# One-hots of a recommendation tower moved to GpSimd, between its gathers

## The chip, the cores and the metric

The kernel runs on 1 core of a Trainium2 chip. The metric is the device time of one execution in microseconds (us), the median of several runs. The core has a matrix engine (PE), a vector engine (DVE), a scalar engine (ACT), GpSimd (POOL) and SyncE (SP), which here only issues transfers.

## The reference

Inputs are 512 samples, each with 16 dense values and 50 ids into 50 tables of 1000 to 125000 rows of 16 floats. For each sample the 50 rows are fetched, the inner products of all 1225 pairs of them are taken, and a three-layer perceptron runs on them:

```
e = stack([tbl_f[ids[:, f]] for f in range(50)], axis=1)      # (512, 50, 16)
gram = einsum('bid,bjd->bij', e, e); z = gram[:, I_IDX, J_IDX]  # pairs i < j
h = concatenate([z, dense_ctx], axis=1)                         # (512, 1241)
h = maximum(h @ W_top1 + b_top1, 0)                             # 512 wide
h = maximum(h @ W_top2 + b_top2, 0)                             # 256 wide
y = h @ W_top3                                                  # (512, 1)
```

Everything is float32.

## The kernel before, in words

The 512 samples are 4 tiles (0 to 3) of 128. A field gets its row in one of three ways.

**Small tables** (26 fields, NS; at most 1280 rows) lie in SBUF as `table`, 128 partitions by R = 10 rows of 16. The id is split into a quotient (the partition) and a remainder. The quotients of all samples are written to DRAM and read back to every partition as `wide` (`load_wide(t)` on SP, two buffers, tile t in t % 2). A comparison of `wide` with the partition's own number, `consts[:, 0:1]`, gives the one-hot matrices `onehot[:, t % 2, field, :]` (128x128 each, `onehots(t, u)`, L510, on DVE, nine fields at a time: three instructions a tile, the last with eight fields). PE multiplies one-hot by table for three fields at a time (`select(t, u)`, L777, u from 0 to 8). DVE multiplies the result with a mask of the remainder (`pick`, L498) and sums it (`fold`, L482) into `fixed`.

**Two large tables** (NP = 2) go by one-hots too, in tiles 1 to 3, four matrices each (`onehots_large(t, n)`, L519; `select(t, 9)` and `select(t, 10)`, L767).

**The other large tables** are gathered row by row from DRAM by GpSimd's indirect DMA: 24 gathers in tile 0 and 22 in each of tiles 1 to 3, 90 in all, each with 128 samples of one field, into `moving`. Each tile's first 12 are its mid part (the gathers 1 to 12, 25 to 36, 47 to 58 and 69 to 80), the others its late part (tile 2's end with gather 68). Tile 3's late part is cut into three, so that the work can begin on each. Behind every gather GpSimd clears a piece of memory that nobody reads, `spacer`, 128x288 (L300):

```
    if ticks[0]:
        pool.wait_ge(spaced, ticks[0])
    nc.gpsimd.memset(spacer[:], 0.0).then_inc(spaced, 1)
    ticks[0] += 1
```

**Products.** For each tile DVE transposes the small fields (`turn_smalls`, L536), the mid part (`turn_mid`, L542, waits for `mid_gathered[t]`) and the late part (`turn_late`, L558). DVE and ACT copy them onto block diagonals (`copy_mid`, `copy_late`, and on ACT `raise_mid`, `raise_late`, L214, L344, L356). PE multiplies (`product_y(t)`, L792, for the mid part; `product_x(t, part)`, L811, for the late one), DVE and ACT unload the result from PSUM to `z` (`unload_y`, `unload_x`, `unload_pairs`, L220, L225). The first layer is 12 chunks of 4 matmuls for a tile (`chunks`, L818), the sixth of which is the first to need the late part; then ACT's Relu (`hidden`, L383), the second layer on PE (L868, L878) and the third on DVE (`last_layer`, L604).

**The order.** Every engine works through its own instructions strictly in order, and between engines there are semaphores. The order of PE, ACT and DVE is written out by hand at the end of each engine's block (DVE L607 to L752, PE L887 to L942, ACT L392 to L424). SP's order is: the small tables, `load_wide(0)`, the other tables, `load_wide(1)`, weights, `load_wide(2)`, the two large tables, `load_wide(3)`, the rest of the dense input, the result. `load_wide(t)` for t >= 2 waits until the one-hots of tile t - 2 are made, since they read the same buffer.

Of the kernel before, what the change touches and what calls it, by code (L numbers as in the profile page):

```python
# [8 lines left out]
P = 128  # L9
# [26 lines left out]
QP = P // Q  # L36
SPACE = 288
SIDE = 64

# [22 lines left out]
WC = 3 * SC  # L62
# [7 lines left out]

CONSTS = 5 + SPLIT + RL


# [20 lines left out]
def build_tower(nc, quotients, ids, ids_t, extra, small, w1, w2, b2, w3, consts_in, out, *tables):  # L94
# [8 lines left out]
    with ctx:  # L103
# [21 lines left out]
        onehot = sb("onehot", [P, 2, NS, P])  # L125
        large_mask = sb("large_mask", [P, TILES - 1, NP, RL])
        large_hot = sb("large_hot", [P, NP, SPLIT, P])
        picked = sb("picked", [P, 3, SC, D, R])
# [34 lines left out]
        wide_ready = sem("wide_ready")  # L163
        large_ready = sem("large_ready")
        rows_made = sem("rows_made")
        rows_used = sem("rows_used")
# [68 lines left out]
        def _(sp):  # L235
# [51 lines left out]
        @block.gpsimd  # L287
        def _(pool):

            ticks = [0]  # L290

            def gather(t, slot, table, field, landed):

                nc.gpsimd.indirect_dma_start(  # L294
                    moving[:, t, slot, 0:D], None, table,
                    bass.IndirectOffsetOnAxis(ap=ids_sb[:, t, field:field + 1], axis=0),
                ).then_inc(landed, 16)
                if ticks[0]:
# [12 lines left out]
            pool.wait_ge(spaced, TILES * NL - sum(SELECTED))  # L311

        @block.scalar
        def _(act):
# [112 lines left out]
        def _(dve):  # L427
# [27 lines left out]
            def large_masks():  # L455

                dve.wait_ge(folded, unit(0, NSC))
                fields = ids_sb[:, 1:, NS + HALF:NS + HALF + NP]
                quot_l = quot[:, 1:, 0:NP]
                rem_l = rem[:, 1:, 0:NP]  # L460
                step(nc.vector.tensor_scalar(quot_l, fields, -(RL - 1) / 2, 1.0 / RL, ALU.add, ALU.mult))
# [52 lines left out]
            def onehots_large(t, n):  # L514

                dve.wait_ge(wide_loaded[t], 16)
                if SELECTED[t - 1]:
                    dve.wait_ge(rows_made, unit(t - 1, NSC + n + 1))
# [121 lines left out]
            fold(1, 1)  # L640
            fold(1, 2)
            unload_y(0)
            onehots(1, 2)
            onehots(2, 0)
            onehots(2, 1)
            onehots(2, 2)
            pick(1, 3)
            pick(1, 4)
            turn_late(0, 0)
            pick(1, 5)  # L650
            copy_late(0, 0)
            fold(1, 3)
            fold(1, 4)
            fold(1, 5)
            pick(1, 6)
            pick(1, 7)
            unload_x(0, 0)
            pick(1, 8)
            unload_pairs(0)
            fold(1, 6)  # L660
            fold(1, 7)
            pick(1, 9)
            fold(1, 8)
            fold(1, 9)
            onehots_large(2, 0)
            onehots_large(2, 1)
            turn_smalls(1)
            pick(1, 10)
            pick(2, 0)
            fold(1, 10)  # L670
            fold(2, 0)
            pick(2, 1)
            turn_mid(1)
            pick(2, 2)
            onehots(3, 0)
            copy_mid(1)
            fold(2, 1)
            fold(2, 2)
            onehots(3, 1)
            onehots(3, 2)  # L680
            pick(2, 3)
            pick(2, 4)
            fold(2, 3)
            unload_y(1)
            pick(2, 5)
            fold(2, 4)
            fold(2, 5)
            pick(2, 6)
            pick(2, 7)
            fold(2, 6)  # L690
            fold(2, 7)
            pick(2, 8)
            last_layer(0)
            fold(2, 8)
            turn_late(1, 0)
            pick(2, 9)
            copy_late(1, 0)
            pick(2, 10)
            turn_smalls(2)
            pick(3, 0)  # L700
            fold(2, 9)
            fold(2, 10)
            unload_x(1, 0)
            fold(3, 0)
            unload_pairs(1)
            pick(3, 1)
            pick(3, 2)
            fold(3, 1)
            fold(3, 2)
            onehots_large(3, 0)  # L710
            onehots_large(3, 1)
            turn_mid(2)
            pick(3, 3)
            copy_mid(2)
            fold(3, 3)
            pick(3, 4)
            pick(3, 5)
            fold(3, 4)
            fold(3, 5)
            last_layer(1)  # L720
            smalls(3, 6, 7)
# [12 lines left out]
            unload_pairs(2)  # L734
# [20 lines left out]
        def _(pe):  # L755

            def select(t, u):
# [130 lines left out]
            selections(0, 0, 9)  # L888
            selections(1, 0, 5)
            product_y(0)  # L890
            layer0 = first_layer(0)
            chunks(layer0, 4)
            select(1, 5)
            chunks(layer0, 1)
            selections(1, 6, 8)
            product_x(0, 0)
            selections(1, 8, 11)
            select(2, 0)
            chunks(layer0, 5)
            selections(2, 1, 3)  # L900
            chunks(layer0, 2)
            selections(2, 3, 5)
            second_layer(0)
            product_y(1)
            selections(2, 5, 7)
            layer1 = first_layer(1)
            chunks(layer1, 1)
            select(2, 7)
            chunks(layer1, 1)
            selections(2, 8, 11)  # L910
            select(3, 0)
            chunks(layer1, 1)
            select(3, 1)
            chunks(layer1, 1)
            product_x(1, 0)
            select(3, 2)
            chunks(layer1, 7)
            selections(3, 3, 5)
            chunks(layer1, 1)
            select(3, 5)  # L920
            second_layer(1)
            selections(3, 6, 8)
            select(3, 8)
            product_y(2)
            select(3, 9)
# [91 lines left out]
```

## Time and profile before

| | |
|---|---|
| median of 3 runs | 158.98 us (158.74 to 159.48) |
| profiled execution, own time | 159.45 us |
| its span in the profile | 157.3 us |
| busy PE, DVE, ACT, POOL | 127.8, 110.6, 44.4, 124.7 us |
| gathers (L294) | 90, busy 89.3 us |
| clearings (L300) | 90, busy 35.4 us |
| one-hots on DVE (L510) | 12, busy 10.4 us |

A profile comes from one execution, and its times are in microseconds from the start of the span. The 2.15 us between its own time and its span lie around the span. A row of the timeline gives the start, the time to the end of the group, engine, line, operation, what it writes and reads with shapes, and the number of instructions; the bracket gives how long the engine stood idle before it and what ended that.

### The profile page before, as it was taken

The numbers are of one execution on the slowest core, as the hardware profiler recorded it, in microseconds if no ns is written. First come the engines' busy times: TensorE is split into PE (matmuls) and PEld (weight loads), VectorE is DVE, ScalarE is ACT, GpSimd is POOL, SyncE is SP. The second block draws the span as 40 slices with busy tenths as digits, with TensorE's granted clock in tenths as the row PEclk, the third lists the DMA queues.
The fourth block names the chain that finished last, engine by engine and source line by source line (L and its number), as shares of the span: only waits on it lengthen the run. The fifth ranks groups of instructions, "written<-read, shape, count | busy, mean of one in ns | idle before, by whom it ended". The sixth has DMA issues, their size and how long they took to land.

```text
span 157.3 us, 3325 instructions
## 1 busy us (share of the span) xinstructions
PE 127.8 (81%) x1323; PEld 111.9 (71%) x1323; DVE 110.6 (70%) x193; ACT 44.4 (28%) x77; POOL 124.7 (79%) x184
## 2 busy tenths in 40 slices
PE   0007875937698999999999989999995994999992
PEld 0007764827588679978959989886695983899991
DVE  1807899998899989998898894999953019344021
ACT  8930000232205220332071205204422018444020
POOL 2989898898998989899889889898988898982000
PEclk9999998696899999999999999999999999999998
DMA  3199999734380010000000100010000000000000
GB/s 84 35 358 419 442 417 317 279 116 119 125 256 15 6 6 4 10 7 4 10 6 4 10 4 6 11 10 6 4 10 6 4 10 4 10 6 6 0 0 1
DMA packets 6486, 12.40 MB, mean 79 GB/s; under 512 B 2077, under 2 KB 5414, under 8 KB 6342
## 3 DMA queue, kind: packets, MB, share of 16 engines
q1 hardware_dynamic: 3592, 11.46, 19.7%
q0 software_dynamic: 2880, 0.74, 5.6%
q8 instruction: 10, 0.16, 0.5%
q14 instruction: 4, 0.03, 0.1%
HBM read 12.17 MB, written 0.03 MB: 78 GB/s over the span
## 4 chain that ended last, share of the span: by engine, by line
POOL 70%; PE 14%; issue 9%; DMA 3%; ACT 2%; DVE 1%; DVEq 0%
POOL moving L294 50%; POOL spacer L300 20%; PE psm L818 4%; PE gram L811 4%; DMA moving<-tbl,ids_sb 2%; PE gram L818 2%; PE p L818 2%; DMA ids_sb<-in_ids 1%; PE gram L792 1%; PE pt L878 1%; ACT blocks L214 1%; DVE mcols L542 1%; ACT scols L344 0%; PE pt L868 0%; DVE h2w L604 0%
## 5 line engine op out<-in xcount | busy, mean ns | idle before, releaser
L294 POOL DMA_INDIRECT moving<-tbl,ids_sb x90 | 89.3, 992 | 17.4 <-issue 14.6
L777 PE MATMUL psm<-table,onehot 128*128 128x160 f32 x208 | 36.7, 326 | 19.3 <-DVE onehot L510 12.8
L777 PEld LDWEIGHTS psm<-table,onehot 128*128 128x128 f32 x208 | 32.2, 206 | 22.3 <-issue 12.8
L818 PE MATMUL p<-z,w_sb 128*128 128x128 f32 x312 | 39.3, 276 | 2.3 <-DVE z L225 2.3
L818 PEld LDWEIGHTS p<-z,w_sb 128*128 128x128 f32 x312 | 37.1, 192 | 3.6 <-ACT z L225 1.8
L300 POOL MEMSET spacer<- 128x288 f32 x90 | 35.4, 394 | 0.0
L498 DVE TENSOR_TENSOR picked<-psm,mask 128x480 f32<-128x480 f32 (+1 forms) x36 | 22.1, 634 | 4.5 <-PE psm L777 4.2
L214 ACT COPY blocks<-mcols 32x384 f32<-32x384 f32 (+3 forms) x20 | 15.4, 771 | 32.4 <-DVE mcols L542 21.2
L220 DVE COPY z<-gram 63x384 f32<-63x384 f32 (+1 forms) x20 | 9.6, 480 | 17.3 <-PE gram L811 14.0
L482 DVE TENSOR_REDUCE fixed<-picked 128x48 f32<-128x480 f32 (+1 forms) x36 | 21.3, 627 | 0.2
L767 PE MATMUL psm<-large_table,large_hot 125*128 125x400 f32 x48 | 16.9, 501 | 0.0
L220 ACT COPY z<-gram 63x384 f32<-63x384 f32 (+1 forms) x20 | 8.1, 407 | 30.5 <-PE gram L811 21.8
L510 DVE TENSOR_SCALAR onehot<-wide,consts 128x1152 f32<-128x1152 bf16 (+1 forms) x12 | 10.4, 917 | 3.9 <-DMA wide<-quotients 3.9
L767 PEld LDWEIGHTS psm<-large_table,large_hot 125*128 125x128 f32 x48 | 8.8, 190 | 5.9
L214 DVE COPY blocks<-mcols 32x384 f32<-32x384 f32 (+3 forms) x20 | 12.3, 613 | 0.7
L811 PEld LDWEIGHTS gram<-blocks,scols 128*63 128x63 f32 x384 | 11.5, 138 | 1.5 <-ACT scols L356 0.7
L811 PE MATMUL gram<-blocks,scols 128*63 128x52 f32 (+2 forms) x384 | 12.2, 216 | 0.5 <-ACT scols L356 0.5
L536 DVE STREAM_TRANSPOSE scols<-fixed 128x1632 f32<-128x1632 f32 x4 | 12.3, 3084 | 0.0
L792 PE MATMUL gram<-blocks,scols 128*63 128x48 f32 x256 | 9.5, 239 | 3.0 <-ACT scols L344 3.0
L792 PEld LDWEIGHTS gram<-blocks,scols 128*63 128x63 f32 x256 | 9.0, 155 | 4.1 <-issue 4.1
L329 ACT COPY moving<-fixed 128x192 f32<-128x192 f32 x4 | 1.4, 351 | 34.5 <-DVE fixed L482 34.5
L542 DVE STREAM_TRANSPOSE mcols<-moving 128x384 f32<-128x384 f32 x4 | 3.6, 903 | 8.4 <-DMA moving<-tbl,ids_sb 8.4
(50 smaller groups left out, 86.5 us busy)
## 6 DMA issues: line engine op xcount, KB each, us to landing
wide<-quotients SPq DMA_DIRECT2D x4, 896.0 KB, 8.2
w_sb<-in_w SPq DMA_DIRECT2D x1, 3072.0 KB, 17.4
large_table<-tbl SPq DMA_DIRECT2D x2, 781.2 KB
moving<-tbl,ids_sb POOLq DMA_INDIRECT x90, 2.8
table<-in_small SPq DMA_DIRECT2D x1, 720.0 KB, 7.2
table<-in_small SPq DMA_DIRECT2D x1, 640.0 KB, 8.7
w_sb<-in_w SPq DMA_DIRECT2D x1, 512.0 KB
table<-in_small SPq DMA_DIRECT2D x1, 480.0 KB, 5.9
```

Source lines behind the costliest of these rows:

```text
L214: return copy(blocks[QP * q:QP * (q + 1), t % 2, :, a:b, q], mcols[QP * q:QP * (q + 1), t % 2, :, a:b])
L220: return copy(to.rearrange("p k (n j) -> p k n j", n=2), g[:, 1 + a:1 + b].rearrange("p (k h) n j -> p k h n j", h=2)[:, :, h])
L294: nc.gpsimd.indirect_dma_start(moving[:, t, slot, 0:D], None, table, bass.IndirectOffsetOnAxis(ap=ids_sb[:, t, field:field + 1], axis=0),) ...
L300: nc.gpsimd.memset(spacer[:], 0.0).then_inc(spaced, 1)
L482: nc.vector.tensor_reduce(fixed[:, t % 2, UPPER + a:UPPER + b, 0:D], picked_rows(m, b - a, R), AX.X, ALU.add).then_inc(folded, 1)
L498: nc.vector.tensor_tensor(picked_rows(m, k, rows), psm[:, m % 2, 0:k * rows * D].rearrange("p (f r d) -> p f d r", r=rows, d=D), which.uns ...
L536: nc.vector.transpose(scols[:, t % 2, :, 0:MID].rearrange("p j s -> p s j"), fixed[:, t % 2]).then_inc(small_cols, 1)
L767: ins = nc.tensor.matmul(psm[:, m % 2, 0:RL * D], large_hot[0:UNITS, n, q, :], large_table[0:UNITS, n, q, :], start=q == 0, stop=q == SPLI ...
L777: ins = nc.tensor.matmul(psm[:, m % 2, (f - a) * R * D:(f - a + 1) * R * D], onehot[:, t % 2, f, :], table[:, f, :], start=True, stop=True)
L792: ins = nc.tensor.matmul(gram_out(2, WIDE, g, 1, GC), scols[:, t % 2, g, 0:WIDE], blocks[:, t % 2, g, YS:, :], start=True, stop=True)
L811: ins = nc.tensor.matmul(gram_out(0, WIDE, g, a, b), scols[:, t % 2, g, XB:], blocks[:, t % 2, g, a:b, :], start=True, stop=True)
L818: return nc.tensor.matmul(hidden_sums(t, k), w1_sb[:, c, P * k:P * (k + 1)], z[:, t % 2, c, :], start=first, stop=last)
```

## The change

Behind 35 of the 90 gathers GpSimd no longer clears `spacer` but compares two fields (256 columns) of `wide` with the partition's number and writes them to `onehot`. These are tile 1's fields 9 to 25 (behind gathers 13 to 21), all 26 of tile 2 (behind 23 to 35) and all 26 of tile 3 (behind 41 to 53). DVE keeps tile 0's three instructions and tile 1's first, fields 0 to 8. PE waits on `pool_ready` for the fields of GpSimd, and SP's `load_wide(3)` waits for the GpSimd one-hots of tile 1 in place of DVE's. The quotients and remainders of the two large tables get memory of their own. `onehots_large(t, n)` waits for PE only where the tile before used that matrix. The orders of PE, DVE and ACT are written anew. In the cut diff, a line of "..." is left out text.

```diff
+HOT_FIELDS = 2
+HOT_BEGINS = {1: 12, 2: 22, 3: 40}
+FIRST_HOT = {0: 26, 1: 9, 2: 0, 3: 0}
+VECTOR_HOTS = [3, 4, 4, 4]
+def pool_hots(t, b):
+    return sum(-(-(NS - FIRST_HOT[n]) // HOT_FIELDS) for n in range(1, t)) + -(-(b - FIRST_HOT[t]) // HOT_FIELDS) if t else 0
...
             def load_wide(t):
                 if t >= 2:
-                    sp.wait_ge(wide_ready, NWC * (t - 1))
+                    sp.wait_ge(wide_ready, VECTOR_HOTS[t - 2])
+                    if t > 2:
+                        sp.wait_ge(pool_ready, pool_hots(t - 2, NS))
                     sp.wait_ge(large_ready, sum(SELECTED[:t - 1]))
...
             def gather(t, slot, table, field, landed):
...
+                count[0] += 1
+                for tile, began in HOT_BEGINS.items():
+                    first = FIRST_HOT[tile] + HOT_FIELDS * (count[0] - 1 - began)
+                    if FIRST_HOT[tile] <= first < NS:
+                        pool_onehots(tile, first, min(first + HOT_FIELDS, NS))
+                        return
+                clear_spacer()
+
+            def pool_onehots(t, a, b):
+                if a == FIRST_HOT[t]:
+                    pool.wait_ge(wide_loaded[t], 16)
+                    if t == 1:
+                        pool.wait_ge(consts_loaded, 16)
+                    else:
+                        pool.wait_ge(rows_made, unit(t - 2, NSC))
+                nc.gpsimd.tensor_scalar(onehot[:, t % 2, a:b, :],
+                                        wide[:, t % 2, P * a:P * b].rearrange("p (f b) -> p f b", b=P),
+                                        consts[:, 0:1], None, ALU.is_equal).then_inc(pool_ready, 1)
...
-            pool.wait_ge(spaced, TILES * NL - sum(SELECTED))
+            pool.wait_ge(spaced, ticks[0])
...
# ACT
-            place_smalls(2)
             raise_late(1, 0)
             unload_x(1, 0)
+            place_smalls(2)
             unload_pairs(1)
+            hidden(1)
             raise_mid(2)
-            hidden(1)
+            unload_y(2)
             place_smalls(3)
-            unload_y(2)
...
# DVE, first part
             fold(0, 2)
+            fold(0, 3)
             pick(0, 4)
-            onehots(1, 0)
-            onehots(1, 1)
             pick(0, 5)
-            fold(0, 3)
+            onehots_large(1, 0)
...
             fold(0, 8)
+            onehots_large(1, 1)
             large_masks()
+            turn_smalls(0)
+            turn_mid(0)
+            onehots(1, 0)
+            copy_mid(0)
             pick(1, 0)
             pick(1, 1)
-            turn_smalls(0)
-            turn_mid(0)
-            pick(1, 2)
-            copy_mid(0)
-            onehots_large(1, 0)
-            onehots_large(1, 1)
...
-            onehots(1, 2)
-            onehots(2, 0)
-            onehots(2, 1)
-            onehots(2, 2)
...
-            onehots(3, 0)
...
-            onehots(3, 1)
-            onehots(3, 2)
...
# DVE, end of tile 2
             fold(3, 8)
-            unload_y(2)
+            turn_late(2, 0)
+            copy_late(2, 0)
             turn_smalls(3)
-            turn_late(2, 0)
             pick(3, 9)
-            copy_late(2, 0)
+            pick(3, 10)
+            unload_x(2, 0)
             fold(3, 9)
-            smalls(3, 10, 11)
-            unload_x(2, 0)
+            fold(3, 10)
             unload_pairs(2)
...
# PE
                 a, b = field_groups(SC)[u]
-                pe.wait_ge(wide_ready, NWC * t + -(-b // WC))
+                if b <= FIRST_HOT[t] or t == 0:
+                    pe.wait_ge(wide_ready, (VECTOR_HOTS[t - 1] if t else 0) + -(-b // WC))
+                else:
+                    if FIRST_HOT[t]:
+                        pe.wait_ge(wide_ready, VECTOR_HOTS[t])
+                    pe.wait_ge(pool_ready, pool_hots(t, b))
...
             selections(0, 0, 9)
-            selections(1, 0, 5)
+            selections(1, 0, 2)
             product_y(0)
+            selections(1, 2, 4)
             layer0 = first_layer(0)
...
             layer2 = first_layer(2)
             chunks(layer2, 1)
-            select(3, 10)
-            chunks(layer2, 4)
+            selections(3, 5, 7)
+            chunks(layer2, 1)
+            selections(3, 7, 9)
+            chunks(layer2, 1)
+            selections(3, 9, 11)
             product_x(2, 0)
-            chunks(layer2, 7)
+            chunks(layer2, 9)
             second_layer(2)
...
             chunks(layer3, 4)
             product_x(3, 1)
-            chunks(layer3, 5)
+            chunks(layer3, 4)
             product_x(3, 2)
-            chunks(layer3, 2)
+            chunks(layer3, 3)
             second_layer(3)
```

## Rows read from the trace of the kernel before

**Rows 1.** The page's chain of waits, followed back from the end

```profile
POOL 70%; PE 14%; issue 9%; DMA 3%; ACT 2%; DVE 1%; DVEq 0%
```

**Rows 2.** Timeline: the 80th gather, then DVE and PE at tile 3's start

```profile
125.88 0.95 POOL L294 DMA_INDIRECT moving<-tbl,ids_sb  x1 [0.17 <-issue]
...
129.18 0.91 DVE L542 STREAM_TRANSPOSE mcols<-moving 128x384 f32<-128x384 f32 x1 [7.70 <-DMA moving<-tbl,ids_sb]
...
128.64 1.99 PE L878 MATMUL pt<-w_sb,h1t 128*128 128x256 f32 x8
132.66 2.04 PE L792 MATMUL gram<-blocks,scols 128*63 128x48 f32 x64 [2.02 <-ACT scols L344]
```

**Rows 3.** GpSimd's instructions (min/median/max ns; the last: busy us, mean ns)

```profile
L294 POOL DMA_INDIRECT moving<-tbl,ids_sb x90: 950/950/1438, 3.2 to 141.1; - x90
...
L300 POOL MEMSET spacer<- x90: 352/353/867, 4.3 to 142.0; 128x288 f32 x90
...
L1002 POOL MEMSET const-float32-0.0<- 128x1 f32 x1 | 0.1, 99 | 0.2 <-issue 0.2
```

**Rows 4.** Timeline: GpSimd's pairs beside DVE's one-hots, and these

```profile
20.48 1.54 DVE L510 TENSOR_SCALAR onehot<-wide,consts 128x1152 f32<-128x1152 bf16 x2
...
41.63 0.79 POOL L300 MEMSET spacer<- 128x288 f32 x1
42.59 1.30 POOL L294 DMA_INDIRECT moving<-tbl,ids_sb  x1 [0.16 <-issue]
...
44.40 1.20 POOL L294 DMA_INDIRECT moving<-tbl,ids_sb  x1 [0.17 <-issue]
...
41.04 3.74 DVE L510 TENSOR_SCALAR onehot<-wide,consts 128x1024 f32<-128x1024 bf16 x4
...
65.99 1.44 POOL L294 DMA_INDIRECT moving<-tbl,ids_sb  x1 [0.17 <-issue]
...
69.19 0.86 POOL L300 MEMSET spacer<- 128x288 f32 x1
70.21 1.20 POOL L294 DMA_INDIRECT moving<-tbl,ids_sb  x1 [0.16 <-issue]
```

**Rows 5.** The page's groups: DVE's one-hots (busy us, mean ns)

```profile
L510 DVE TENSOR_SCALAR onehot<-wide,consts 128x1152 f32<-128x1152 bf16 (+1 forms) x12 | 10.4, 917 | 3.9 <-DMA wide<-quotients 3.9
```

**Rows 6.** Timeline: GpSimd beside onehots_large

```profile
93.33 1.28 DVE L519 TENSOR_TENSOR large_hot<-wide,consts 128x512 f32<-128x512 bf16 x2
...
93.72 0.36 POOL L300 MEMSET spacer<- 128x288 f32 x1
94.25 1.19 POOL L294 DMA_INDIRECT moving<-tbl,ids_sb  x1 [0.17 <-issue]
```

**Rows 7.** What GpSimd's new waits look at (first: landing of `wide`)

```profile
DMA to landing us min/median/max: 4.9/8.2/17.0
...
14.28 0.35 SPq L252 DMA_DIRECT2D wide<-quotients  x1
...
25.50 1.05 DVE L498 TENSOR_TENSOR picked<-psm,mask 128x480 f32<-128x480 f32 x2
...
51.59 0.81 PE L777 MATMUL psm<-table,onehot 128*128 128x160 f32 x4
```

**Rows 8.** Timeline: the end of tile 2; then two groups of DVE

```profile
111.42 0.96 DVE L558 STREAM_TRANSPOSE mcols<-moving 128x416 f32<-128x416 f32 x1
...
114.35 0.61 ACT L356 ACTIVATE scols<-mcols,consts 128x352 f32<-128x352 f32 x1
...
117.72 2.05 PE L811 MATMUL gram<-blocks,scols 128*63 128x52 f32 x64
121.47 6.49 PE L818 MATMUL p<-z,w_sb 128*128 128x128 f32 x56 [1.70 <-DVE z L225]
...
L498 DVE TENSOR_TENSOR picked<-psm,mask 128x480 f32<-128x480 f32 x32 | 20.3, 653 | 4.5 <-PE psm L777 4.2
...
L536 DVE STREAM_TRANSPOSE scols<-fixed 128x1632 f32<-128x1632 f32 x4 | 12.3, 3084 | 0.0
```

More of the change, by code:

```diff
@@ L126, in build_tower @@
         large_mask = sb("large_mask", [P, TILES - 1, NP, RL])
+        large_quot = sb("large_quot", [P, TILES, NP])
+        large_rem = sb("large_rem", [P, TILES, NP])
         large_hot = sb("large_hot", [P, NP, SPLIT, P])
@@ L164, in build_tower @@
         large_ready = sem("large_ready")
+        pool_ready = sem("pool_ready")
         rows_made = sem("rows_made")
@@ L290, in _ @@
             ticks = [0]
+            count = [0]
             def gather(t, slot, table, field, landed):
@@ L297, in gather, with clear_spacer @@
                 ).then_inc(landed, 16)
+                count[0] += 1
[15 more added lines that the diff above has]
+                                        consts[:, 0:1], None, ALU.is_equal).then_inc(pool_ready, 1)
+            def clear_spacer():
                 if ticks[0]:
@@ L455, in large_masks @@
             def large_masks():
-                dve.wait_ge(folded, unit(0, NSC))
                 fields = ids_sb[:, 1:, NS + HALF:NS + HALF + NP]
-                quot_l = quot[:, 1:, 0:NP]
-                rem_l = rem[:, 1:, 0:NP]
+                quot_l = large_quot[:, 1:]
+                rem_l = large_rem[:, 1:]
                 step(nc.vector.tensor_scalar(quot_l, fields, -(RL - 1) / 2, 1.0 / RL, ALU.add, ALU.mult))
@@ L516, in onehots_large @@
                 dve.wait_ge(wide_loaded[t], 16)
-                if SELECTED[t - 1]:
+                if SELECTED[t - 1] > n:
                     dve.wait_ge(rows_made, unit(t - 1, NSC + n + 1))
@@ L629, in _ @@
             fold(0, 8)
+            onehots_large(1, 1)
             large_masks()
+            turn_smalls(0)
+            turn_mid(0)
+            onehots(1, 0)
+            copy_mid(0)
             pick(1, 0)
             pick(1, 1)
-            turn_smalls(0)
-            turn_mid(0)
-            pick(1, 2)
-            copy_mid(0)
-            onehots_large(1, 0)
-            onehots_large(1, 1)
             fold(1, 0)
             fold(1, 1)
+            unload_y(0)
+            pick(1, 2)
+            pick(1, 3)
             fold(1, 2)
-            unload_y(0)
-            onehots(1, 2)
-            onehots(2, 0)
-            onehots(2, 1)
-            onehots(2, 2)
-            pick(1, 3)
-            pick(1, 4)
+            fold(1, 3)
+            smalls(1, 4, 5)
+            pick(1, 5)
             turn_late(0, 0)
-            pick(1, 5)
+            pick(1, 6)
             copy_late(0, 0)
-            fold(1, 3)
-            fold(1, 4)
+            pick(1, 7)
             fold(1, 5)
-            pick(1, 6)
-            pick(1, 7)
-            unload_x(0, 0)
             pick(1, 8)
-            unload_pairs(0)
             fold(1, 6)
             fold(1, 7)
+            fold(1, 8)
+            unload_x(0, 0)
+            unload_pairs(0)
+            turn_smalls(1)
             pick(1, 9)
-            fold(1, 8)
+            pick(1, 10)
             fold(1, 9)
+            fold(1, 10)
             onehots_large(2, 0)
             onehots_large(2, 1)
[L667 to L671, printed above, removed]
+            smalls(2, 0, 1)
             pick(2, 1)
             turn_mid(1)
+            fold(2, 1)
+            copy_mid(1)
             pick(2, 2)
-            onehots(3, 0)
-            copy_mid(1)
-            fold(2, 1)
+            pick(2, 3)
             fold(2, 2)
-            onehots(3, 1)
-            onehots(3, 2)
-            pick(2, 3)
-            pick(2, 4)
             fold(2, 3)
             unload_y(1)
-            pick(2, 5)
-            fold(2, 4)
-            fold(2, 5)
+            last_layer(0)
+            smalls(2, 4, 6)
+            turn_late(1, 0)
             pick(2, 6)
+            copy_late(1, 0)
             pick(2, 7)
@@ L691, in _ @@
             fold(2, 7)
[L692 to L695, printed above, removed]
+            smalls(2, 8, 9)
+            unload_x(1, 0)
+            unload_pairs(1)
+            turn_smalls(2)
             pick(2, 9)
-            copy_late(1, 0)
+            onehots_large(3, 0)
+            fold(2, 9)
+            onehots_large(3, 1)
             pick(2, 10)
-            turn_smalls(2)
             pick(3, 0)
-            fold(2, 9)
+            turn_mid(2)
             fold(2, 10)
-            unload_x(1, 0)
+            copy_mid(2)
             fold(3, 0)
-            unload_pairs(1)
             pick(3, 1)
-            pick(3, 2)
+            last_layer(1)
             fold(3, 1)
[L709 to L712, printed above, removed]
+            smalls(3, 2, 3)
+            unload_y(2)
             pick(3, 3)
-            copy_mid(2)
+            pick(3, 4)
             fold(3, 3)
-            pick(3, 4)
-            pick(3, 5)
             fold(3, 4)
-            fold(3, 5)
-            last_layer(1)
-            smalls(3, 6, 7)
+            smalls(3, 5, 7)
             pick(3, 7)
@@ L888, in _ @@
             selections(0, 0, 9)
-            selections(1, 0, 5)
+            selections(1, 0, 2)
             product_y(0)
+            selections(1, 2, 4)
             layer0 = first_layer(0)
+            chunks(layer0, 1)
+            select(1, 4)
+            chunks(layer0, 1)
+            selections(1, 5, 7)
+            chunks(layer0, 1)
+            select(1, 7)
+            chunks(layer0, 2)
+            select(1, 8)
+            product_x(0, 0)
+            selections(1, 9, 11)
             chunks(layer0, 4)
-            select(1, 5)
+            selections(2, 0, 2)
             chunks(layer0, 1)
[L895 to L900, printed above, removed]
+            selections(2, 2, 4)
             chunks(layer0, 2)
-            selections(2, 3, 5)
+            product_y(1)
             second_layer(0)
-            product_y(1)
-            selections(2, 5, 7)
             layer1 = first_layer(1)
             chunks(layer1, 1)
-            select(2, 7)
-            chunks(layer1, 1)
-            selections(2, 8, 11)
+            selections(2, 4, 6)
+            chunks(layer1, 4)
+            selections(2, 6, 9)
+            product_x(1, 0)
+            select(2, 9)
+            chunks(layer1, 6)
+            select(2, 10)
             select(3, 0)
             chunks(layer1, 1)
[L913 to L920, printed above, removed]
+            selections(3, 1, 3)
             second_layer(1)
-            selections(3, 6, 8)
-            select(3, 8)
             product_y(2)
-            select(3, 9)
+            select(3, 3)
+            select(3, 4)
             layer2 = first_layer(2)
             chunks(layer2, 1)
-            select(3, 10)
-            chunks(layer2, 4)
+            selections(3, 5, 7)
[3 more added lines that the diff above has]
+            selections(3, 9, 11)
             product_x(2, 0)
-            chunks(layer2, 7)
+            chunks(layer2, 9)
             second_layer(2)
```

## The prediction

> **What bounds the kernel now.** I read the busy times first (the small table): GpSimd 124.7 us, PE 127.8, DVE 110.6 of a span of 157.3. Values so close name no bound, so the chain of waits comes next. It puts 70% on GpSimd, which is the gathers (L294) and the clearings behind them (L300), and 14% on PE [rows 1]. The timeline near the end tells where the chain passes from one to the other. The 80th gather is the last of tile 3's mid part. It starts at 125.88 and DVE turns its data at 129.18, after 7.70 us in which DVE only waited for that transfer; PE starts the last product_y at 132.66 after 2.02 us of waiting, and from there on it does tile 3's work to the end [rows 2]. So every microsecond by which the 80th gather moves, the end moves too, as long as PE, ACT and DVE are done with tile 2 in time: PE ends tile 2's second layer at 128.64 + 1.99 = 130.63, which leaves 2.0 us of slack.
>
> GpSimd's pace: a gather takes 0.950 us at the least and in the median, a clearing 0.353, and 0.17 lies between [rows 2, 3]; 1.47 us a pair. The largest are 1.438 and 0.867: some pairs are held up by DVE. While DVE makes four one-hots (tile 1's last and tile 2's three, 41.04 to 44.78), a clearing takes 0.79, a gather 1.30 and one 1.20 [rows 4]. The clearing of 0.79 is followed by a gather that is no shorter for it, so time added to a pair stays in the sum; no reserve between gathers takes it up.
>
> **The change, part by part.**
>
> *The swap on GpSimd.* 9 pairs for tile 1 (behind gathers 13 to 21), 13 for tile 2 (23 to 35) and 13 for tile 3 (41 to 53) get a one-hot instruction of two fields, 128x256 (one of them 128x128), instead of a 128x288 clearing; 35 in all, all ahead of gather 80. 55 clearings stay. The price is 35 x (c - 0.353), with c the new instruction's duration, which this trace does not show on GpSimd. Bounds from the nearest rows: the clearing of one element takes 0.099, of 288 it takes 0.353 [rows 3], so an element costs 0.00089; 256 of them at that rate give 0.099 + 0.227 = 0.325, sum -1.0 us. If reading and writing an element cost one such step each, it is 0.099 + 2 x 0.227 = 0.553, sum +7.0. DVE reads and compares at most 1152 elements in 0.917, which is 0.0008 an element and below the clearing's rate [rows 5], so reading need not cost a step of its own. I go by the row that the instruction is nearest to, the clearing itself, and take c = 0.36, sum +0.2, with both ends kept for the range.
>
> The Trainium skill (GPSIMD Engine Reference, section 3.1) puts a GpSimd body with at most two operations on an element at 1.03 cycles an element, and its best simple loops of more at 1.8, at 1.2 GHz; 256 elements would be 0.22 and 0.38 us. That is an estimate by the page, and no row here decides between the two; with the 0.10 of a one-element clearing added it gives 35 x (0.32 - 0.353) = -1 or 35 x (0.48 - 0.353) = +4.4 us.
>
> *What leaves DVE.* 8 of 12 one-hot instructions go (2 for tile 1, 3 each for tiles 2 and 3), 8 x 0.917 = 7.3 us of DVE [rows 5]. That itself is worth nothing at the end, since DVE stands idle for 7.70 us ahead of turn_mid(3) [rows 2]. What counts is what they did to GpSimd [rows 4]: the four from 41.04 added 0.44 + 0.35 + 0.25, tile 3's second and third 0.51 + 0.25 at 69.19 and 70.21; of the 0.49 on the gather at 65.99 I give half to tile 3's first, since copy_mid(1) follows it within the same gather. That is 1.80 + 0.25, taken as 2.0 us to be gained. Below, 1.0, if copies of DVE that now fall elsewhere hit more pairs; above, 2.8, if they hit fewer.
>
> *A new collision.* onehots_large on DVE has two inputs in SBUF. Two of them, from 93.33 to 94.61, left the clearing at 93.72 at 0.36 and stretched the gather at 94.25 from 0.95 to 1.19 [rows 6]. A clearing reads nothing; the new instruction reads `wide`. Two of the six such instructions (tile 1's) now stand where GpSimd makes tile 1's one-hots, two (tile 2's) near tile 3's, and each can hold one new instruction for its own 0.64. No hit is 0, two whole ones are +1.3; I take 0.4. The Trainium skill (SBUF — State Buffer, "Who interferes with whom") has it that a DVE instruction with two SBUF inputs contends with a GpSimd instruction that reads SBUF and not with one that only writes. By that rule a clearing is spared and a one-hot is not; the trace agrees on the clearing (0.36).
>
> *GpSimd's new waits.* Behind a waiting one-hot stands every later gather, so a wait there would go straight to the end. Tile 1's first (after gather 13, at about 24 us) needs wide[1], which DVE used at 20.48 without a wait [rows 4]. Tile 2's first (after gather 23, at about 38.7) needs wide[2], issued at 14.28 and landed no more than 17.0 later, 31.3, and tile 0's selections, whose last picks ended at 26.55 [rows 7]. Tile 3's first (after gather 41, which starts at 65.99) needs wide[3], which SP now issues after tile 1's GpSimd one-hots (gather 21, at about 36), 17 us more at most; and tile 1's small selections, the last of which PE ended at 52.40 [rows 7]. Cost 0 for all three, with 3, 7 and 13 us of cover. PE in turn waits for GpSimd's one-hots: tile 2's are complete at about 58.5 and tile 3's at about 87, each two fields per 1.47 us from 38.7 and 67 on, while PE's selections of that tile come about when they do now; the first need two of the 13. Cost 0. SP has only load_wide(3) and small later transfers behind its new wait: cost 0.
>
> *The orders of PE, ACT and DVE.* Tile 1's first selections now come about with tile 0's transposes, and product_x(1) and product_x(2) ahead of more first-layer chunks. Only tile 2's end matters. Now: DVE turns tile 2's late part (ending with gather 68) at 111.42, ACT is done with it at 114.96, product_x(2,0) waits for PE until 117.72, PE stands idle 1.70 us for the unload, and its last seven chunks take 6.49 [rows 8]. New: product_x(2,0) can start at 115.0 and two chunks run beside the unload; but DVE now has turn_smalls(3) (3.08), two picks and two folds (0.65 each) and the unloads (no more than the 1.70) behind its copies, which end by 114.3 like ACT's: 114.3 + 3.1 + 2.6 + 1.7 = 121.7, where it is 121.5 now. Seven chunks, Relu and second layer follow as now, so tile 2 ends at about 130.8, still 1.9 us ahead of product_y(3), and gather 68 moves along with gather 80. Worth 0, cost 0; if DVE comes to turn_late(2,0) more than 1.9 us late, the rest is paid in full.
>
> *The tail.* product_x(3,2) comes one chunk (6.49 / 7 = 0.9 us) earlier. PE's sum of work behind product_y(3) is the same: 0, at worst 0.9 if the last gathers are not turned by then.
>
> **The sum**, against the profiled execution's own 159.45 (span 157.3 and 2.15 around it): +0.2 - 2.0 + 0.4 = -1.4, so 158.05. The median of the runs shown, 158.98, lies 0.47 lower, and by it the forecast is 157.6. A measurement can tell about 0.5% (0.8 us) here.
>
> **Rivals.**
> *Slower: the new instruction costs clearly more than the clearing.* Its place is the 35 pairs. Break-even is at 35 x (c - 0.353) = 1.6, c = 0.399; from 0.422 it is slower by over 0.5%. At 0.50: 158.98 + 5.1 - 1.6 = 162.5; at the upper bound 0.553: 164.4. For it: two operands to read (data and the comparison value), a conversion from bf16, and no row that shows GpSimd reading at the clearing's rate. Against: DVE's row, where reading and converting costs nothing beyond the element [rows 5]. Chance 0.35. The Trainium skill (same page on GpSimd, section 4.1) says of elementwise work on GpSimd "~2× slower for 2-input ops" and "1-input is roughly line-rate": the first would be this rival, the second is my forecast.
> *About the same.* c between 0.376 and 0.422, price and gains cancel: 158.98 to within 0.8. Chance 0.15.
> *DVE or PE late.* The new orders eat the slack of 1.9 us and the 1.4 gained, and the gain is gone: 159.0. For it: the reckoning above leaves under 2 us. Against: 7.3 us of DVE's work is gone ahead of it. It decides from 3.3 us of delay. Chance 0.06.
> *A shorter pair does not pay.* A gather sooner than 0.35 after the one before might take longer than 0.950; no row shows a pair below 1.47. If the 35 gathers give the relief back: 159.0. Chance 0.03.
>
> **How the numbers follow.** The forecast (c up to 0.376) covers 156.2 to 158.2, taken 157.6, chance 0.41. The cases about 159 hold 0.24, of which I give 0.02 to each side. Faster by over 0.5%: 0.43; within: 0.20; slower: 0.37. The range for 8 in 10 goes from 155.8 (c 0.325, -1.0, with a relief of 2.6 less 0.4) to 162.9 (c 0.51, +5.5 - 1.6); the forecast's own is 156.2 to 158.2.
>
> **What would show it.** GpSimd's new instruction at 0.33 to 0.38 and a pair of 1.45 to 1.50 confirm the first step; 0.45 and more with a pair above 1.55 refute it. Gather 80 should start at about 124.5 (125.88 - 1.4), and DVE's one-hot instructions be 4. DVE should still wait for the transfer ahead of turn_mid(3): if not, the chain has passed to PE or DVE. A wait of GpSimd for a DMA or for PE ahead of a one-hot would refute the zero for its waits. The argument is wrong at its root if the time moves while gather 80 does not.

## The result and the profile after

The changed kernel takes 182.43 us (median of 4; 180.78 to 185.8) against 159.23 for the kernel before, a ratio of 1.142 (95% interval 1.133 to 1.152). The forecast was 157.6, the range ended at 162.9. Ratios, here and below, leave out executions in a slower state, here the one of 185.8. The profiled execution took 182.78 us, its span is 180.9.

First the page after: span, busy times, chain of waits by engine, GpSimd's three groups (busy us, mean ns, idle before). Then come a row of the view by shape and one of the view of the tile `onehot` (min/median/max ns).

```profile
span 180.9 us, 3321 instructions
PE 134.2 (74%) x1323; PEld 117.7 (65%) x1323; DVE 102.1 (56%) x185; ACT 44.5 (25%) x77; POOL 145.8 (81%) x184
...
POOL 72%; PE 13%; issue 8%; DMA 3%; ACT 1%; DVE 1%; POOLq 0%; DVEq 0%
...
L314 POOL DMA_INDIRECT moving<-tbl,ids_sb x90 | 91.3, 1015 | 17.6 <-issue 14.9
...
L334 POOL TENSOR_SCALAR onehot<-wide,consts 128x256 f32<-128x256 bf16 (+1 forms) x35 | 33.7, 963 | 1.3
...
L342 POOL MEMSET spacer<- 128x288 f32 x55 | 20.7, 377 | 0.0
...
L334 POOL TENSOR_SCALAR onehot<-wide,consts 128x128 f32<-128x128 bf16 x1 | 0.6, 632 | 0.0
...
L334 POOL TENSOR_SCALAR onehot<-wide,consts x35: 632/948/1352, 23.5 to 107.9; 128x256 f32<-128x256 bf16 x34, 128x128 f32<-128x128 bf16 x1
```

GpSimd's busy time grew by 21.1 us, DVE's fell by 8.5, and the chain is still GpSimd's, 72% against 70% [rows 1]. A comparison of two fields takes 0.948 us in the median, where a clearing took 0.353 [rows 3]. Now GpSimd's timeline after, in the stretch of tile 2's one-hots, and one of the instructions while DVE makes its own one-hot:

```profile
46.04 1.03 POOL L314 DMA_INDIRECT moving<-tbl,ids_sb  x1 [0.17 <-issue]
47.10 0.95 POOL L334 TENSOR_SCALAR onehot<-wide,consts 128x256 f32<-128x256 bf16 x1
48.23 1.03 POOL L314 DMA_INDIRECT moving<-tbl,ids_sb  x1 [0.18 <-issue]
...
30.23 1.35 POOL L334 TENSOR_SCALAR onehot<-wide,consts 128x256 f32<-128x256 bf16 x1
```

A pair is 48.23 - 46.04 = 2.19 us instead of 1.47: +0.60 for the instruction, +0.08 for the gather behind it (1.03 against 0.95), +0.04 ahead of the instruction. Thirty-five pairs are 25.2 us. What becomes of them is seen at gather 80, DVE's turn of its data and PE's product_y(3) in the profile after, where [rows 2] shows the same before. The last three rows are windows: their bounds and length, the busy time of PE, PE's weight loads, DVE, ACT and GpSimd, then PE's granted clock (PEclk), DMA share and GB/s:

```profile
148.55 0.96 POOL L314 DMA_INDIRECT moving<-tbl,ids_sb  x1 [0.16 <-issue]
...
151.06 0.91 DVE L583 STREAM_TRANSPOSE mcols<-moving 128x384 f32<-128x384 f32 x1 [8.15 <-DMA moving<-tbl,ids_sb]
...
149.99 1.99 PE L908 MATMUL pt<-w_sb,h1t 128*128 128x256 f32 x8
154.54 3.38 PE L822 MATMUL gram<-blocks,scols 128*63 128x48 f32 x64 [2.56 <-ACT scols L386]
...
151.00:154.50 3.50, 0.99 (x5) 0.53 (x3) 3.19 (x7) 2.42 (x4) 3.17 (x5) 1.00 0.06 5
154.50:158.00 3.50, 3.46 (x65) 3.40 (x65) 0.63 (x3) 1.42 (x4) 3.00 (x6) 0.56 0.08 7
158.00:178.00 20.00, 19.64 (x298) 18.43 (x298) 5.87 (x18) 5.63 (x17) 6.28 (x10) 0.99 0.03 4
```

Gather 80 starts 22.67 us later, product_y(3) 21.88 later (DVE turns the data of gather 80 2.5 us after its start instead of 3.3), and the span is 23.6 longer. Most of the remaining 1.7 is product_y(3) itself: 3.38 instead of 2.04, since PE's granted clock was 0.56 in that stretch after 2.56 us of idling.

### The profile page after: what moved, and what is told of

It is laid out like the page before. It is cut to its first block, busy times and chain, and to the rows that moved or that the text cites. A ratio compares the mean times of both kernels' runs of the same rounds, so it can differ in the third digit from the quotient of the medians.

```text
span 180.9 us, 3321 instructions
## 1 busy us (share of the span) xinstructions
PE 134.2 (74%) x1323; PEld 117.7 (65%) x1323; DVE 102.1 (56%) x185; ACT 44.5 (25%) x77; POOL 145.8 (81%) x184
## 4 chain that ended last, share of the span: by engine, by line
POOL 72%; PE 13%; issue 8%; DMA 3%; ACT 1%; DVE 1%; POOLq 0%; DVEq 0%
POOL moving L314 45%; POOL onehot L334 19%; POOL spacer L342 9%; PE psm L848 3%; PE gram L841 3%; PE gram L822 2%; PE p L848 1%; PE gram L848 1%; DMA moving<-tbl,ids_sb 1%; DMA ids_sb<-in_ids 1%; ACT blocks L231 1%; PE pt L908 1%; DVE mcols L583 1%; PE pt L898 0%; ACT scols L386 0%
## 5 line engine op out<-in xcount | busy, mean ns | idle before, releaser
L314 POOL DMA_INDIRECT moving<-tbl,ids_sb x90 | 91.3, 1015 | 17.6 <-issue 14.9
L807 PE MATMUL psm<-table,onehot 128*128 128x160 f32 x208 | 35.7, 323 | 24.5 <-DVE onehot L551 20.8
L848 PEld LDWEIGHTS p<-z,w_sb 128*128 128x128 f32 x312 | 37.3, 192 | 2.3 <-issue 1.7
L334 POOL TENSOR_SCALAR onehot<-wide,consts 128x256 f32<-128x256 bf16 (+1 forms) x35 | 33.7, 963 | 1.3
L822 PE MATMUL gram<-blocks,scols 128*63 128x48 f32 x256 | 12.7, 282 | 15.6 <-ACT scols L386 15.6
L822 PEld LDWEIGHTS gram<-blocks,scols 128*63 128x63 f32 x256 | 12.2, 201 | 16.8 <-issue 16.8
L342 POOL MEMSET spacer<- 128x288 f32 x55 | 20.7, 377 | 0.0
L841 PEld LDWEIGHTS gram<-blocks,scols 128*63 128x63 f32 x384 | 12.7, 149 | 4.1 <-ACT scols L398 3.0
L841 PE MATMUL gram<-blocks,scols 128*63 128x52 f32 (+2 forms) x384 | 13.4, 228 | 2.5 <-ACT scols L398 2.5
L231 DVE COPY blocks<-mcols 32x384 f32<-32x384 f32 (+3 forms) x20 | 10.1, 506 | 0.7
L908 PE MATMUL pt<-w_sb,h1t 128*128 128x256 f32 x32 | 9.5, 449 | 0.1
```

The costliest lines, as they stand in the source:

```text
L231: return copy(blocks[QP * q:QP * (q + 1), t % 2, :, a:b, q], mcols[QP * q:QP * (q + 1), t % 2, :, a:b])
L314: nc.gpsimd.indirect_dma_start(moving[:, t, slot, 0:D], None, table, bass.IndirectOffsetOnAxis(ap=ids_sb[:, t, field:field + 1], axis=0),) ...
L334: nc.gpsimd.tensor_scalar(onehot[:, t % 2, a:b, :], wide[:, t % 2, P * a:P * b].rearrange("p (f b) -> p f b", b=P), consts[:, 0:1], None, ...
L807: ins = nc.tensor.matmul(psm[:, m % 2, (f - a) * R * D:(f - a + 1) * R * D], onehot[:, t % 2, f, :], table[:, f, :], start=True, stop=True)
L822: ins = nc.tensor.matmul(gram_out(2, WIDE, g, 1, GC), scols[:, t % 2, g, 0:WIDE], blocks[:, t % 2, g, YS:, :], start=True, stop=True)
L841: ins = nc.tensor.matmul(gram_out(0, WIDE, g, a, b), scols[:, t % 2, g, XB:], blocks[:, t % 2, g, a:b, :], start=True, stop=True)
```

## Experiments

Each was timed beside runs of the kernel before (medians 158.5 to 159.2). Theory: the loss is the length of the 35 pairs, on the chain of the gathers. Rivals: the new orders; waits or collisions.

**The swap with the old orders** (e1; the lines are against the kernel before).

```diff
 # the changed kernel, with the orders of PE, ACT and DVE of the kernel before
-            onehots(1, 1)
-            onehots(1, 2)
... (and onehots(2, 0) to onehots(3, 2))
```

> The swap alone: GpSimd makes the 35 one-hots, but PE, ACT and DVE keep the orders of the kernel before (DVE's eight one-hots are just left out). Theory 1 (price): an exchanged pair of GpSimd takes 2.19 instead of 1.47 us (one-hot 0.95, the gather behind it 1.03), 35 x 0.72 = 25.2 us on the chain of the gathers, less 1 to 2 us for pairs that DVE no longer holds up; the orders don't matter. Time 180 to 184. Theory 2 (orders): 5 us or more of the loss come from the new orders, so the old ones give 177 or less.

182.78 us, ratio 1.153 (1.144 to 1.162), gather 80 at 148.62, 0.07 from the changed kernel. The orders have no part in the loss that can be told from the noise.

**Clearing in place** (e2).

```diff
-                nc.gpsimd.tensor_scalar(onehot[:, t % 2, a:b, :], wide[...], consts[:, 0:1], None, ALU.is_equal).then_inc(pool_ready, 1)
+                nc.gpsimd.memset(onehot[:, t % 2, a:b, :], 0.0).then_inc(pool_ready, 1)
```

> The changed kernel, but each of the 35 one-hot instructions is a clearing of the same 128x256 of onehot, with the same waits and the same semaphore; the comparison is left out, so the small fields of tiles 1 to 3 from 9 on come out as zero. Theory 1 (price): all of the loss is what the reading and comparing instruction costs; with 0.325 instead of 0.353 for 35 clearings (-1.0) and 2.0 us of held-up pairs gone, 156 to 158. Theory 2 (orders, waits or collisions): the time stays above 162, since waits, orders and DVE's work are as in the changed kernel.

157.23 us, ratio 0.988 (0.985 to 0.992). Everything is as in the changed kernel, waits and orders too, except for what the instruction does. The view of the tile `onehot`, then GpSimd, DVE and PE in the timeline:

```profile
L334 POOL MEMSET onehot<- x35: 219/326/833, 23.4 to 83.3; 128x256 f32 x34, 128x128 f32 x1
...
46.67 0.95 POOL L314 DMA_INDIRECT moving<-tbl,ids_sb  x1 [0.16 <-issue]
47.63 0.33 POOL L334 MEMSET onehot<- 128x256 f32 x1
48.12 1.24 POOL L314 DMA_INDIRECT moving<-tbl,ids_sb  x1 [0.16 <-issue]
...
122.74 0.95 POOL L314 DMA_INDIRECT moving<-tbl,ids_sb  x1 [0.16 <-issue]
...
125.10 0.93 DVE L581 STREAM_TRANSPOSE mcols<-moving 128x384 f32<-128x384 f32 x1 [3.93 <-DMA moving<-tbl,ids_sb]
...
130.66 2.04 PE L820 MATMUL gram<-blocks,scols 128*63 128x48 f32 x64 [0.42 <-ACT scols L384]
```

Gather 80 is 3.14 us earlier than before [rows 2], of which 35 x (0.353 - 0.326) = 0.9 is the shorter clearing; the other 2.2 are time for which DVE no longer holds up GpSimd's pairs. The end gains 2.1: PE now waits 0.42 instead of 2.02 and is the bound. All of the changed kernel's loss, 182.4 against 157.2, is thus in the one instruction: its own time and what it adds to the gather behind it.

**Prices** (e3): the kernel before with ten forms in turn behind its gathers.

```diff
-                nc.gpsimd.memset(spacer[:], 0.0).then_inc(spaced, 1)
+                form().then_inc(spaced, 1)   # one of nine; in the tenth place nothing
```

> The kernel before with nine other instructions and one empty place in turn behind its gathers, all writing to spacer only: comparison bf16 to fp32 of 256 columns with the partition's number, clearing of 256, the same comparison from fp32, comparison with a constant, copy bf16 to fp32, copy fp32 to fp32, nothing, comparison of 64 columns, multiplication instead of comparison, product of two fp32 tensors. By the changed kernel's trace (0.948 for 256, 0.632 for 128 columns) a comparison costs 0.31 + 0.00247 a column, so 64 columns 0.47. If reading is what costs, the copies take 0.9 too; if the operation does, they take 0.35 to 0.5. If the pointer to the partition's number is the fixed part, the constant saves 0.1 to 0.3. If a gather needs a spacing, the gather behind the empty place takes over 0.95; if not, 0.95. Time: about 9 x 0.6 us more on average per ten pairs gives 165 to 190.

Durations (min/median/max ns) by form, from the view of one tile; L296 is the change's own instruction, L299 compares with a constant, L304 multiplies, L305 has two tensors as inputs:

```profile
L296 POOL TENSOR_SCALAR spacer<-quot_t,consts x9: 948/959/1305, 7.5 to 156.3; 128x256 f32<-128x256 bf16 x9
L297 POOL MEMSET spacer<- x9: 326/330/334, 9.7 to 158.8; 128x256 f32 x9
L298 POOL TENSOR_SCALAR spacer<-table,consts x9: 940/942/1497, 11.2 to 160.3; 128x256 f32<-128x256 f32 x9
L299 POOL TENSOR_SCALAR spacer<-quot_t x9: 878/878/883, 14.3 to 162.5; 128x256 f32<-128x256 bf16 x9
L300 POOL CAST spacer<-quot_t x9: 408/408/409, 16.3 to 164.6; 128x256 f32<-128x256 bf16 x9
L301 POOL COPY spacer<-table x9: 401/407/700, 17.9 to 166.1; 128x256 f32<-128x256 f32 x9
L303 POOL TENSOR_SCALAR spacer<-quot_t,consts x9: 460/471/1414, 20.7 to 169.0; 128x64 f32<-128x64 bf16 x9
L304 POOL TENSOR_SCALAR spacer<-quot_t,consts x9: 949/950/960, 23.0 to 170.7; 128x256 f32<-128x256 bf16 x9
L305 POOL TENSOR_TENSOR spacer<-table x9: 624/624/847, 25.1 to 172.8; 128x256 f32<-128x256 f32 x9
```

In a copy, reading costs next to nothing: with its conversion it takes 0.408, only 0.08 above the clearing of as many columns. The pointer to the partition's number costs 0.08 (0.959 against 0.878), less than the 0.1 to 0.3 that I had expected; the conversion costs nothing. Comparing or multiplying makes no difference (0.959, 0.950). What is dear is the form, tensor with scalar: 0.47 at 64 columns, 0.63 at 128 (in the changed kernel) and 0.95 at 256 are 0.0025 us a column and 0.31 fixed, and two whole tensors are cheaper (0.624). The run took 188.07 us, inside its wide range. Behind an empty place the gather stays at 0.94 to 0.95 in all nine places, so it needs no spacing; here is one of them, and below it a gather behind the change's own instruction (1.03):

```profile
19.74 0.94 POOL L310 DMA_INDIRECT moving<-tbl,ids_sb  x1 [0.30 <-issue]
...
28.07 1.03 POOL L310 DMA_INDIRECT moving<-tbl,ids_sb  x1 [0.17 <-issue]
```

**An instruction in between** (e5).

```diff
-                nc.gpsimd.tensor_scalar(..., consts[:, 0:1], None, ALU.is_equal)
+                nc.gpsimd.tensor_tensor(..., consts[:, 0:1].unsqueeze(2).to_broadcast([P, b - a, P]), ALU.subtract)
```

> The changed kernel, but GpSimd's 35 instructions subtract the partition's number (a broadcast second tensor) from the two fields of wide, tensor to tensor, in place of the comparison; the one-hots of these fields are left out, their values are differences. It puts the price between the clearing in place (0.344) and the comparison (0.95): a product of 256 fp32 columns took 0.624, the gather behind it 0.98, so a pair is about 1.83. Theory 1 (the chain of gathers is all that counts, linear in the pair): 35 x 0.36 = 12.6 above 1.47 each, less 2 for held-up pairs, 159.2 + 10.6 = 169.8, in 168 to 172. Theory 2 (the loss is due to something that the comparison alone does, such as late one-hots that PE waits for): no more than 162 or as much as 178.

166.43 us, ratio 1.049 (1.043 to 1.055): below the range that I gave, since the gather behind this form took 0.96 and the pair was 46.40 - 44.64 = 1.76, not 1.83 (first two rows). With the measured pair, 35 x 0.29 = 10.2, less the 2.2 of e2, puts gather 80 at 133.9. It started at 132.15, so the loss follows the length of the pairs, but the relief from DVE was 3.9 here and isn't a fixed amount.

```profile
44.64 0.96 POOL L314 DMA_INDIRECT moving<-tbl,ids_sb  x1 [0.16 <-issue]
...
46.40 0.96 POOL L314 DMA_INDIRECT moving<-tbl,ids_sb  x1 [0.16 <-issue]
...
138.01 3.56 PE L823 MATMUL gram<-blocks,scols 128*63 128x48 f32 x64 [2.82 <-ACT scols L387]
```

**Fewer pairs** (e8: tile 1's 9; e11: tile 3's 13, behind gathers 45 to 57), with the old orders. DVE keeps the one-hots of the other tiles; the lines are against e1.

```diff
-HOT_BEGINS = {1: 12, 2: 22, 3: 40}
-FIRST_HOT = {0: 26, 1: 9, 2: 0, 3: 0}
+HOT_BEGINS = {1: 12}                      # e11: {3: 44}
+FIRST_HOT = {0: 26, 1: 9, 2: NS, 3: NS}   # e11: {0: 26, 1: NS, 2: NS, 3: 0}
```

> The kernel before with the swap for tile 1's fields 9 to 25 alone: 9 pairs in place of 35, the orders of before, DVE keeps the one-hots of tiles 2 and 3. Theory 1 (linear in the number of pairs): 9 x 0.72 = 6.5, less about 0.5 of held-up pairs, 164.5 to 166. Rival (the loss comes from tiles 2 and 3, or from slack used up only once): below 162, or over 168.

> The same 13 pairs with the 77 clearings kept. Now gather 80 is on the chain: 13 x 0.72 = 9.4, less 1 of held-up pairs, 158.8 + 8.4 = 167, in 166 to 168.5. If the same swap is hidden here as well, or costs under 5, the chain of gathers isn't what makes it dear.

e8: 166.14 us, ratio 1.047 (1.040 to 1.053), just above the expectation. e11: 167.7, ratio 1.059 (1.054 to 1.063), within it. In e8 two of the nine instructions met DVE's two-input and one-hot instructions (in e11 one of thirteen took 1.64); GpSimd's timeline of e8:

```profile
34.25 1.74 POOL L334 TENSOR_SCALAR onehot<-wide,consts 128x256 f32<-128x256 bf16 x1
...
39.42 2.04 POOL L334 TENSOR_SCALAR onehot<-wide,consts 128x256 f32<-128x256 bf16 x1
```

**No clearings** (e4, repeated as e4b and e4c).

```diff
-                if ticks[0]:
-                    pool.wait_ge(spaced, ticks[0])
-                nc.gpsimd.memset(spacer[:], 0.0).then_inc(spaced, 1)
-                ticks[0] += 1
```

> The kernel before with no clearing behind any gather. If clearings are dead time, gathers come every 1.12 us, gather 80 starts about 28 us sooner and the bound passes to DVE and PE: 145 to 155. If a gather needs its spacing (the rival of the prediction that a shorter pair doesn't pay), the gathers get longer or hold DVE up, and the time is 158 or more.

> The same kernel as e4_no_clearing, again, on the same chip as e9_tile1_no_clearing and with more rounds, to narrow its interval and to compare the two: 154 to 157, 2 to 3% below the kernel before. If the first time was chance, it is 158 or more.

155.89, 155.55 and 155.05 us; ratios 0.974 (0.964 to 0.983), 0.977 (0.971 to 0.982) and 0.978 (0.975 to 0.981). This beats both kernels. My expectation for e4 (145 to 155, with a gather every 1.12 us and gather 80 about 28 us sooner) was too hopeful. The chain of e4b, its gathers, gather 80 and PE's product_y(3):

```profile
PE 67%; DVE 14%; DMA 6%; issue 5%; ACT 5%; SPq 1%; DVEq 0%; ACTq 0%
...
L294 POOL DMA_INDIRECT moving<-tbl,ids_sb x90: 941/947/1820, 3.0 to 117.7; - x90
...
105.20 0.95 POOL L294 DMA_INDIRECT moving<-tbl,ids_sb  x1 [0.30 <-issue]
...
129.06 2.04 PE L787 MATMUL gram<-blocks,scols 128*63 128x48 f32 x64 [0.39 <-ACT scols L339]
```

The gathers go at 1.25 us, not 1.12, because the time of issue between them is 0.30 where it was 0.17; gather 80 starts 20.7 us earlier, and GpSimd has left the chain. Only 3 of the 20.7 us arrive at the end, as PE is the bound beyond.

**The swap where gathers have slack** (e9: e8 without clearings; e10: e11 without clearings).

```diff
-                clear_spacer()
```

> As e8_tile1_only, but with nothing behind the other 81 gathers. Without clearings gather 80 started at about 106.4, some 18 us before it is needed; 9 pairs of 2.19 instead of 1.25 bring it to about 115, still in time. So if only the chain of gathers makes the swap dear, it is free here, and DVE's 1.8 us less in the crowded stretch from 20 to 45 us can give up to 1: 153.5 to 156, at or below the kernel without clearings. Rival: tile 1's fields come late for PE (complete at about 38 us) and it waits, 157 or more.

> The kernel before with nothing behind 77 gathers and the one-hots of tile 3 alone on GpSimd, 13 pairs behind gathers 45 to 57; the orders of before. In e9_tile1_no_clearing the swap cost 6 us although gather 80 came in time, because the 9 slow pairs lie on tile 0's late gathers: DVE stood 5.75 us at its turn for gather 24. Theory (a slow pair costs only where a later gather is then late for its tile): 13 slow pairs from gather 45 on bring gather 46 to about 61 (needed at 79) and gather 80 to about 118 (needed at 125), so all are hidden, and DVE has 2.4 us less: 153.5 to 156, the same as without clearings or up to 1 less. Rival (the instruction costs elsewhere too, by holding DVE or by PE waiting for it): 157.5 or more.

> The kernel before without clearings once more, beside e10_tile3_no_clearing on one chip: 154 to 157.

e9: 162.0 us, ratio 1.020 (1.016 to 1.025). My theory's range (153.5 to 156) failed; the rival's held, but not its reason, since it isn't PE that waits for one-hots. Gather 80 starts at 114.0, early enough, but the 9 slow pairs lie on tile 0's late gathers. The chain of e9 goes through them to gather 24, whose data landed 6.5 us after its start at 42.38; DVE stands 5.75 us for it. Then PE, after waits of 3.98 and 1.00 us, needs 3.66 us for product_x(0,0). First e9's chain, its DVE and its PE, then PE in e4b:

```profile
42.38 6.51 DMA moving<-tbl,ids_sb
...
48.91 0.95 DVE L598 STREAM_TRANSPOSE mcols<-moving 128x416 f32<-128x416 f32 x1 [5.75 <-DMA moving<-tbl,ids_sb]
...
52.49 3.66 PE L854 MATMUL gram<-blocks,scols 128*63 128x52 f32 x64 [1.00 <-ACT scols L397]
...
47.82 2.05 PE L806 MATMUL gram<-blocks,scols 128*63 128x52 f32 x64
```

So product_x(0,0) starts 4.7 us later than in e4b and lasts 1.6 longer, with a granted clock of 0.50 from 52.4 to 57.5, the lower of the two levels (1.2 GHz). At product_y(3) the delay has grown to 7.4. Gather 80 and product_y(3) of e10:

```profile
117.00 0.95 POOL L314 DMA_INDIRECT moving<-tbl,ids_sb  x1 [0.30 <-issue]
...
130.06 2.04 PE L834 MATMUL gram<-blocks,scols 128*63 128x48 f32 x64 [0.41 <-ACT scols L385]
```

e10: 155.84 us, ratio 0.978 (0.973 to 0.982), the same as e4c beside it. 13 of these instructions cost nothing that can be measured where no gather behind them is due, and the three one-hot instructions (2.4 us in e4b) that DVE no longer makes are worth nothing either.

In one table, with gather 80's start, product_y(3)'s start and the span of each profiled run:

| kernel | pairs changed, us each | gather 80 | product_y(3) | span |
|---|---|---|---|---|
| before | 0 | 125.88 | 132.66 | 157.3 |
| after | 35, 2.19 | 148.55 | 154.54 | 180.9 |
| e1, old orders | 35, 2.19 | 148.62 | 155.51 | 180.4 |
| e5, subtract | 35, 1.76 | 132.15 | 138.01 | 164.5 |
| e2, clear in place | 35, 1.45 | 122.74 | 130.66 | 155.2 |
| e8, tile 1 | 9, 2.19 | 132.73 | 139.60 | 164.1 |
| e11, tile 3 | 13, 2.19 | 134.01 | 140.38 | 164.9 |
| e9, tile 1, no clearings | 9, 2.19 | 114.00 | 136.49 | 161.0 |
| e10, tile 3, no clearings | 13, 2.19 | 117.00 | 130.06 | 154.3 |
| e4b, no clearings | 0 | 105.20 | 129.06 | 153.6 |

Where clearings are kept, the span less gather 80's start lies between 30.9 and 32.5 us; without them it is 37.3 to 48.4, and something else sets the end.

## Why the prediction was wrong

**The failed step is the price of the swap on GpSimd**, c = 0.36 with 0.325 and 0.553 as its bounds. It measured 0.948 (median), and the pair grew by another 0.12 that the sum did not have: 25.2 us in place of +0.2. Both ends were built from the clearing, as if an instruction cost what its columns cost to write and at most to read. The runs show reading nearly free (e3: 0.408 for a copy) and the tensor-with-scalar form at 0.0025 a column, 2.8 times the clearing's 0.00089. The comfort taken from DVE's row [rows 5] said nothing of GpSimd. An operation on an engine that had never run it there has no upper bound from another operation of that engine; the range should have been left open upward, and the slower rival, with its break-even at 0.399 rightly placed but capped at 164.4, deserved most of the chance. The prediction's own sign against it (0.45 and more, with a pair above 1.55) came out as 0.948 and 2.19. The two figures taken from The Trainium skill (GPSIMD Engine Reference, section 3.1), 0.32 and 0.48 for this instruction, both lie far under the 0.948 of the trace. Of its section 4.1, "1-input is roughly line-rate", on which the forecast leaned, doesn't hold for this one-input comparison; the copy's 0.408 lies between the two figures. "~2× slower" is said there of two inputs, and this comparison is slower than that: 0.948 for 256 columns against DVE's 0.917 for up to 1152 [rows 5], about 4.5 times as long a column.

**The bound** was right: the chain of gathers carries each added microsecond to the end. Gather 80 moved by 22.67, the end by 23.6.

**What leaves DVE**: forecast 2.0 us (1.0 to 2.8). e2 gives 2.2. In the changed kernel 25.2 - 22.7 = 2.5 is what is left after the collisions' 0.8, so the relief is about 3.3, above the upper end. Right in kind, sized too low; net of collisions 2.5 against 1.6, which softened the loss.

**The collision**: forecast 0.4. In the changed kernel GpSimd's comparisons sum to 33.7 us, 0.8 above 34 x 0.948 + 0.632. Two that met onehots_large on DVE, at 25.68 and 105.50, took 1.11 and 1.13, together 0.35 more, which is what was forecast. Another 0.40 is the one beside DVE's remaining one-hot (30.23), a meeting that the prediction had not counted. e8 shows two hit by 0.8 and 1.1.

**GpSimd's waits, at zero**: right. L334's idle time is 1.3 us over 35 instructions, 0.04 each.

**Orders, at zero**: right at the end (e1 against the changed kernel). The new orders leave a hole early on, PE's 8.88 us for DVE's one remaining one-hot of tile 1 (timeline of the profile after), which the chain of gathers covers.

```profile
31.48 3.54 PE L807 MATMUL psm<-table,onehot 128*128 128x160 f32 x12 [8.88 <-DVE onehot L551]
```

**The sum's other terms together**: with the instruction as cheap as a clearing (e2), gather 80 came 3.1 us earlier, which would give 159.2 - 3.1 = 156.1, and 157.2 was measured. PE was done with tile 2 at 130.66 - 0.42 = 130.24, only 0.4 earlier than before (130.63). The prediction used the slack of 2.0 us as cover against delays and did not say that it also caps the gain: the end can't move by much more. Its forecast of 1.4 stays below the cap. The loss is all in the first term.

**"A shorter pair does not pay"** is refuted by e4, e4b and e4c: pairs of 1.25 leave the gather at 0.95 and the kernel 2.2 to 2.6% faster.

## What to carry to other kernels

Before work moves to an engine, price that very form of instruction there, in the place it will have; a neighbouring form bounds nothing (0.33, 0.41, 0.62 and 0.95 us for 256 columns on one engine). Multiply by the count on the chain before looking at what the move relieves. And ask first whether filler on the bounding engine is needed at all: here removing it gave what the swap was after, and with it gone 13 of the swapped instructions came free.

## What was not expected of the hardware

- GpSimd's tensor-with-scalar instruction costs more than tensor-with-tensor of the same size (0.95 against 0.62 at 256 columns), and the same for compare and multiply. Why was not tried.
- A gather behind such an instruction takes 1.03 instead of 0.95 (1.01 behind the multiplication); behind a clearing or nothing it takes 0.94 to 0.96, behind a copy 0.97 to 0.98, behind a product of two tensors 0.99 (medians, e3). The gathers ahead of a tile's first such instruction stay at 0.95 to 0.96 (13, 23 and 41 in the changed kernel).
- PE's clock: product_y(3) took 3.38 and 3.56 us after 2.56 and 2.82 us of idling (changed kernel, e5), a granted clock of 0.56 in the former's stretch, near the lower of the two levels (1.2 GHz); after 2.02 and 1.92 us (before, e1) it took 2.04 at full clock. In these runs the longer wait ahead of PE cost 1.3 to 1.5 us more than itself, and 1.6 at product_x(0,0) in e9 (after 3.98 and 1.00 us). That the wait is the cause was not tested.
